# One more block product split in seven, in the last two groups of a mixture-of-ranks kernel

## What is computed

```python
x2 = einsum('bct,bcd->bdt', x, weights[condition])        # 64x64 matrix chosen per b
xf = x2.reshape(-1, 1024)                                 # 4096 rows
scores = xf @ Wr.T                                        # 64 experts
top_vals, top_idx = top_k(scores, 16)
G = scatter(softmax(top_vals), top_idx)                   # 4096 x 64, 16 non-zero
h = einsum('nd,krd->nkr', xf, A)                          # 4096 x 1024
out = einsum('nkr,kdr->nd', h * G[:, :, None], B)         # 4096 x 1024
return x + 2.0 * out
```

## Time and profile before

| what | value |
|---|---|
| median of 3 runs | 707.24 us |
| the profiled execution | 707.46 us, its span 705.7 us |
| TensorE busy | 700.4 us, 99% |
| VectorE busy | 568.8 us, 81% |
| ScalarE busy | 292.2 us, 41% |
| granted TensorE clock | 0.999 of full |
| HBM traffic | 306 GB/s over the span |

### The profile page before, as it was taken

The page is one execution under the profiler, slowest core; times in us unless marked ns, Lnnn a source line. Parts: engine busy times, 40 slices in busy tenths (PEclk is TensorE's granted clock), DMA queues, the critical chain, the costliest instruction groups (busy, mean ns, idle before and its releaser), DMA issues.

```text
span 705.7 us, 11098 instructions
## 1 busy us (share of the span) xinstructions
PE 700.4 (99%) x3822; PEld 608.5 (86%) x3822; DVE 568.8 (81%) x1022; ACT 292.2 (41%) x541; POOL 15.8 (2%) x22
## 2 busy tenths in 40 slices
PE   8999999999999999999999999999999999999998
PEld 8888888888888888988999888898899988888897
DVE  5888998897757899889795867987668496699885
ACT  5575554534535541444333542242334364233220
POOL 0000000100000000010000000001000000000100
PEclk9999999999999999999999999999999999999999
DMA  8976679787899998979989775868769987666886
GB/s 314 405 291 279 211 281 401 229 261 268 332 382 417 415 359 290 406 255 325 388 312 412 285 271 189 301 247 245 248 274 372 380 311 258 199 217 211 228 329 239
DMA packets 68937, 212.35 MB, mean 301 GB/s; under 512 B 10706, under 2 KB 13394, under 8 KB 68242
## 3 DMA queue, kind: packets, MB, share of 16 engines
q1 hardware_dynamic: 64802, 204.30, 78.0%
q0 software_dynamic: 2304, 4.20, 3.9%
q10 hardware_dynamic: 1776, 3.15, 1.2%
HBM read 150.80 MB, written 65.01 MB: 306 GB/s over the span
## 4 chain that ended last, share of the span: by engine, by line
PE 99%; DMA 1%; DVE 0%; issue 0%; DVEq 0%
PE Pb L755 40%; PE Pb L788 29%; PE Pb L809 13%; PE Cb L737 8%; PE S L852 4%; PE Pb L831 3%; DMA xc<-in_wts 1%; PE S L844 1%; PE T L907 0%; PE T L913 0%; PE Pb L771 0%; PE Cb L866 0%; PE S L866 0%; PE T L866 0%; DVE Q L1212 0%
## 5 line engine op out<-in xcount | busy, mean ns | idle before, releaser
L755 PE MATMUL Pb<-Op,Wt 128*128 128x512 f32 x888 | 214.2, 391 | 0.0
L755 PEld LDWEIGHTS Pb<-Op,Wt 128*128 128x128 f32 x888 | 165.4, 188 | 33.9
L788 PE MATMUL Pb<-Wt,Op 128*128 128x512 f32 x744 | 179.7, 391 | 0.0
L788 PEld LDWEIGHTS Pb<-Wt,Op 128*128 128x128 f32 x744 | 138.1, 188 | 28.1 <-DVE Op L1212 0.4
L1212 DVE TENSOR_TENSOR Q<-Pb,Q 128x512 f32<-128x512 f32 (+1 forms) x105 | 92.8, 901 | 27.9 <-issue 17.5
L1212 DVE TENSOR_TENSOR Op<-R,Op 128x512 fp32r<-128x512 f32 x100 | 66.6, 686 | 23.4 <-ACT Op L945 23.3
L755 PE MATMUL Pb<-Ox,Wt 128*128 128x512 f32 x300 | 75.3, 390 | 0.0
L998 ACT COPY R<-Cb 128x512 f32<-128x512 f32 x60 | 35.1, 587 | 91.2 <-PE Cb L737 91.2
L755 PEld LDWEIGHTS Pb<-Ox,Wt 128*128 128x128 f32 x300 | 56.0, 188 | 11.5
L945 ACT CAST Op<-R 128x512 fp32r<-128x512 f32 x100 | 58.3, 622 | 17.3 <-DVE R L1212 10.4
L1212 DVE TENSOR_TENSOR Cq<-Pb,Cq 128x1024 f32<-128x1024 f32 (+1 forms) x46 | 44.5, 966 | 24.3 <-issue 10.4
(11 more groups left out here) (118 smaller groups left out, 688.9 us busy)
## 6 DMA issues: line engine op xcount, KB each, us to landing
Wt<-Wd SPq DMA_DIRECT2D x201, 512.0 KB, 6.5
Wd<-Wt SPq DMA_DIRECT2D x56, 512.0 KB, 5.1
xc<-in_x SPq DMA_DIRECT2D x24, 512.0 KB, 5.4
Q<-in_x SPq DMA_DIRECT2D x16, 512.0 KB, 5.3
out<-Q SPq DMA_DIRECT2D x8, 1024.0 KB, 4.8
BR<-in_B SPq DMA_DIRECT2D x4, 1024.0 KB, 8.5
Q<-in_x SPq DMA_DIRECT2D x16, 256.0 KB, 5.6
out<-in_x SPq DMA_DIRECT2D x16, 256.0 KB, 5.9
```

Source lines behind the costliest of these rows:

```text
L755: t = e.matmul(Pb[:, j, :], Wt[:, k, a, 128 * c:128 * c + 128], part((USES1[m], s, c), z), start=fresh and (c, a, z) == (0, 0, 0), stop=(c ...
L788: t = e.matmul(Pb[:, i, :], part((USES2[m], s, c), a)[:, 128 * i:128 * i + 128], Wt[:, k, z, :], start=fresh and (c, a, z) == (0, 0, 0), s ...
```

## The change

P4 in groups 2 and 3 is made as seven products of 256 x 256 x 256 (`FOUR`, `four`). Its operand T4 gets the seven forms: the four sums are written to `u` in stage P6 (`sum_y` with `four`), and there are seven T4 splits instead of four, two of them in stage P4. Its seven weights (level 8) are made in group 2's first half, from a further load of A into `raws[2]` in group 1's last stage. Since the seven products take over the banks that hold P7's values, VectorE first adds these to the result in `base_four` (two banks after P7's second step, one after its fourth, the last one with product 0), and drains all seven products (`drain_four`). The gates of q1 move from P4's steps to the first four steps of Q2. Q2's products in those groups use P2's three banks.

```diff
+FOUR = (2, 3)
+LEVEL = (4, 6, 0, 7, 8)
-           7: [8, 9, 10, 12, 13, 14, 20]}
+           7: [8, 9, 10, 12, 13, 14, 20], 8: [3, 4, 5, 6, 7, 13, 14]}
...
+    if m == 5 and s in FOUR:
+        return [("T4", k) for k in ((0,), (1, 2), (3,), (4,))[j]]
...
+    if s in FOUR:
+        return [("T4", j + 5) if j < 2 else ("G12", j - 2)]
...
+def banks_two(s, m):
+    return BANK1 if m == 0 and s in FOUR else BANK2
...
+                        if (s, m, i) == (1, 6, 0):
+                            e.wait_ge(v_made, 28)
+                            e.dma_start(raws[2], A[4:8, :, 512:1024].rearrange("j p n -> p j n")).then_inc(l_b[4], 16)
...
+                if m == 0 and s in FOUR and k in (0, 1, 3):
+                    if k:
+                        e.wait_ge(*{1: (v_p2, p4_done(s, 5)), 3: (v_prod["P4"], 4 * s + 2)}[k])
+                    else:
+                        e.wait_ge(v_p2, p4_done(s, 4))
...
+            def four(s, k):
+                n = used_first(s, 6, k)
+                at = n % NW
+                e.wait_ge(v_lo["T4"], t4_done(s, k))
+                e.wait_ge(l_t[at], w_landed(n))
+                e.wait_ge(v_p2, p4_done(s, {0: 1, 1: 1, 2: 3, 3: 3, 4: 6, 5: 7, 6: 8}[k]))
+                for j in range(2):
+                    for c in range(2):
+                        for a, z in ((0, 0), (0, 1), (1, 0)):
+                            t = e.matmul(Pb[:, BANK2[k], 256 * j:256 * j + 256],
+                                         Wt[:, at, a, 256 * j + 128 * c:256 * j + 128 * c + 128],
+                                         part(("T4", s, k), z)[:, c, :],
+                                         start=k in (0, 1, 3) and (j, c, a, z) == (0, 0, 0, 0),
+                                         stop=(c, a) == (1, 1), skip_group_check=True)
+                t.then_inc(p_two, 1)
...
+                if name == "t1" and four:
+                    e.wait_ge(v_t4, s + 2)
+                    e.wait_ge(v_lo["S4"], split_done("S4", s - 1, 6))
+                    if s == 2:
+                        e.wait_ge(*stored(8, 3))
+                        e.wait_ge(*stored(8, 6))
...
+            def drain_four(s, r):
+                e.wait_ge(p_two, form_done(s, 8, r))
+                e.wait_ge(v_p2, p4_done(s, {0: 1, 1: 3, 2: 5, 3: 4, 4: 7, 5: 6, 6: 8}[r]))
+                P, to = Pb[:, BANK2[r], :].rearrange("p (j n) -> p j n", n=256), first2(r, 0)
+                if r < 5:
+                    add(to, P, to, v_p2)
+                else:
+                    add(to, P, to, v_prod["P4"], n=2)
+                if r == 0:
+                    add(Cq[:, 0, 3, :], Pb[:, 3, :], Cq[:, 0, 3, :], v_p2)
+
+            def base_four(s, j):
+                if j == 1:
+                    e.wait_ge(a_prod["P1"], 4 * s + 4)
+                    add(Cq[:, 0, 0:2, :], Pb[:, 0:2, :], Cq[:, 0, 0:2, :], v_p2)
+                elif j == 3:
+                    add(Cq[:, 0, 2, :], Pb[:, 2, :], Cq[:, 0, 2, :], v_p2)
...
+                            if s in FOUR:
+                                sum_y(s, SUMS2[j], True)
...
-                            gated(s, 3, j, 1)
-                            if s:
+                                if name == "G12":
+                                    lo(name, s, c)
+                            if j < 4:
+                                gated(s, 3, j, 1)
+                            if s and s not in FOUR:
                                 gated(s, 1, j, 0)
...
-                        if m or s not in ONE:
+                        if m == 6 and s in FOUR:
+                            drain_four(s, j)
+                        elif m or s not in ONE:
                             drain_first(s, m, j)
+                        if m == 5 and s in FOUR:
+                            base_four(s, j)
...
                             if m == 0 and c < 4:
                                 gated(s, 0, c, 0)
+                                if s in FOUR:
+                                    gated(s, 1, c, 0)
```

More of the change, by code:

```diff
@@ L79, in steps_first @@
 def steps_first(s, m):
-    return 7 if m == 0 and s in ONE else 4
+    return 7 if m == 0 and s in ONE or m == 6 and s in FOUR else 4
 def step_first(m, j):
@@ L93, in first_use, with fours @@
 def first_use(m):
-    return min(s for s in range(NS) if (s in ONE if m == 7 else m in TWO[s]))
+    return min(s for s in range(NS) if (s in ONE if m == 7 else s in FOUR if m == 8 else m in TWO[s]))
 def ones(s):
     return sum(r in ONE for r in range(s))
+def fours(s):
+    return sum(r in FOUR for r in range(s))
 def cond_step(s, m, i):
@@ L179, in places @@
                     spare.extend(at["y21", s, c] for c in ((0, 1, 5, 6, 7) if j == 6 else (j,) if FORMS[j][0] == "t" else ()))
+                elif m == 6 and s in FOUR:
+                    spare.append(at["T4", s, j])
                 elif j == 3:
@@ L206, in tile_done @@
 def tile_done(s, m, j):
-    return 49 * s + 7 * m - 7 * ones(s + (m > 0)) + (j + 1 if j < 3 else 7)
+    return 49 * s + 7 * m - 7 * ones(s + (m > 0)) - 7 * fours(s) + (j + 1 if j < 3 else 7)
 def chunk_done(s, m, c):
@@ L225, in form_done @@
 def form_done(s, m, k):
-    return 7 * (ones(s) if m == 7 else ones(s + 1)) + 7 * (level_before(s, TWO[s][0]) if m == 7 else level_before(s, m)) + k + 1
+    of_first = ones(s + (m != 7)) + fours(s + (m < 7))
+    return 7 * of_first + 7 * level_before(s, TWO[s][0] if m > 6 else m) + k + 1
 def level_before(s, m):
@@ L237, in y21_done, with t4_done, ysum_done, p2_done @@
     return 4 * s + 4 * ones(s) + c + 1
+def t4_done(s, k):
+    return 4 * s + 3 * fours(s) + k + 1
+def ysum_done(s, name, four):
+    return 4 * (ones(s + four) + fours(s)) + SUMS2.index(name) + 1
+def p2_done(s, n):
+    return 3 * ones(s) + 8 * fours(s) + n
+def p4_done(s, n):
+    return 3 * ones(s + 1) + 8 * fours(s) + n
+def banks_two(s, m):
+    return BANK1 if m == 0 and s in FOUR else BANK2
 def split_done(name, s, c):
@@ L420, in weight2 @@
             c, n = [(0, 0), (1, 0), (1, 1), (0, 0), (0, 1), (1, 0), (1, 1)][k]
-            if m == 7:
+            if m > 6:
                 c, n = n, c
@@ L470, in source @@
                 return quarter(y(1, 0, 4) if FORMS1[c][0] == "b" else Cq[:, 3, :, :], FORMS1[c])
+            if name == "T4" and s in FOUR:
+                return quarter(y(1, 0, 4) if FORMS[c][0] == "b" else u[:, :, :], FORMS[c])
             if name == "S2":
@@ L507, in operand_used @@
                 return (p_score, 7 * s + 1) if FORMS1[c][0] == "b" else (p_two, form_done(s, 7, c))
+            if name == "T4" and s in FOUR:
+                return p_two, form_done(s, 8, c)
             if name in USES1:
@@ L521, in bank_read @@
             if not second and m == 1 and s in ONE:
-                return ((v_p2, 3 * ones(s) + 1), (v_out, out_done(s - 1, 6, 6)), (v_p2, 3 * ones(s) + 3),
+                return ((v_p2, p2_done(s, 1)), (v_out, out_done(s - 1, 6, 6)), (v_p2, p2_done(s, 3)),
                         (a_prod["P2"], 4 * s + 4))[j]
@@ L527, in bank_read @@
                 m, second = (6, False) if second else (m - 1, False)
+            if second and m == 0 and s in FOUR:
+                return ((v_prod["P4"], 4 * s + 4) if j == 1 else in_output(s, 0, {0: 1, 2: 5, 3: 6}[j]))
             if second and m in TWO[s]:
@@ L650, in _ @@
                                 made_store(k, MADE_AT[k].index(step - 1))
+                        if s == 2 and step - 1 in MADE_AT[8]:
+                            made_store(8, MADE_AT[8].index(step - 1))
                         if (s, step) == (1, 9):
@@ L824, in one @@
                 elif k == 6:
-                    e.wait_ge(v_p2, 3 * ones(s) + 2)
+                    e.wait_ge(v_p2, p2_done(s, 2))
                 else:
@@ L880, in _ @@
                                 score_pieces(s)
+                            continue
+                        elif m == 6 and s in FOUR:
+                            four(s, j)
                             continue
@@ L1020, in wait_y21 @@
                 else:
-                    e.wait_ge(v_ysum, 4 * ones(s) + SUMS2.index(FORMS1[c]) + 1)
+                    e.wait_ge(v_ysum, ysum_done(s, FORMS1[c], False))
             def hi_first(name, s, c):
@@ L1038, in hi_first @@
                     e.wait_ge(v_t3, s + 1)
+                elif name == "T4" and s in FOUR and FORMS[c][0] == "t":
+                    e.wait_ge(v_ysum, ysum_done(s, FORMS[c], True))
                 elif name == "T4":
@@ L1128, in _ @@
                                 made_hi(k, MADE_AT[k].index(step))
+                        if s == 2 and step in MADE_AT[8]:
+                            made_hi(8, MADE_AT[8].index(step))
                         if m == 0 and s in ONE:
@@ L1411, in drain_first @@
                     if s in ONE:
-                        e.wait_ge(v_p2, 3 * ones(s + 1))
+                        e.wait_ge(v_p2, p2_done(s, 3))
                     to = Cq[:, 1, j + 1 - n:j + 1, :]
@@ L1498, in _ @@
```

(2 more changed lines are left out.)

47 lines of the change are left out of this document (28 added, 19 removed).

## The result

The changed kernel takes 717.99 us, the median of four runs (717.61 to 718.91), against 707.72 us of the kernel before in the same comparison: a ratio of 1.0149, with a 95% interval of 1.0134 to 1.0164. The profiled execution took 718.16 us with a span of 716.4 us.

A forecast was written before the change was run, and what follows sets the result against it. TensorE's instruction stream was taken to bound the kernel. Group 2 +3.6, group 3 +4.7 and early group 2 +0.1 made +8.4 us on the profiled 707.46; median 0.2 lower, 715.6 us, range 711 to 720.

The forecast's parts named there:

- Bound and direction: Whole kernel: TensorE's stream is the time, 1.6 us of columns to gain, new waits cost more; slower given 0.92.
- the price read from P2: P4's seven products priced by P2's row: 84 narrow matmuls in 10.08 us, 1.44 us per product.
- P4's walk: P4, groups 2 and 3: VectorE's queue added up operation by operation; stage 14.52 us, 3.62 us more per group.
- The forecast stalls: P4: TensorE waits for drains before products 2, 4 and 5, of 2.1, 1.9 and 0.35 us.
- Q2 of group 3: q1's gates delay drain 4, so product 6 stalls 1.1 us; no stall in group 2.
- Making seven weights: Group 2's first half: added splits and sums push P1's second drain; value 0.05 us, bounds 0 and 0.5.
- Stores, the load of A and the units: Added DMA traffic hides behind SyncE's nine-unit, 13 us lead against 10.1 us landing; value 0, bounds 0 and 1 us.
- The clock: Rival: idle gaps in P4 drop TensorE to the 1.2 GHz level; about 725 us, chance 0.06.
- The rival's price: Clock rival in P4: products 2 to 6 all slow, 14.4 us, +5 us per group.
- The sum: Whole kernel: group 2 +3.6, group 3 +4.7, early part of group 2 +0.1, together +8.4 us, giving 715.6 us.

The follow-up runs named there:

- Experiment 5: Changed kernel, A loaded early, most of VectorE's splits, sums, gates and base additions around P4 cut to about 8 columns, drains whole: 706.16 us, ratio 0.998.
- experiment 1: Changed kernel with the 1 MB load of A issued earlier, in group 1's Q5 stage instead of Q3: 716.92 us.
- experiment 8: Kernel before plus only the 1 MB load of A at group 1's Q3 start, into a buffer nobody reads: 709.19 us, ratio 1.0026.
- experiment 3: Changed kernel with q1's gates put back into P4's first four steps: 724.12 us, ratio 1.0231.
- experiment 4: Changed kernel with each product's drain placed ahead of that step's split, sum and gate in P4's VectorE order: 718.63 us.
- experiment 6: Changed kernel with the early load of A and q1's and q3's gates of groups 2 and 3 on GpSimd instead of VectorE: 719.98 us.

## Why the prediction came out as it did

**Bound and direction.** Right. TensorE's stream was the time, 1.6 us of columns was all there was to gain, and the first waits in mid-run cost more. Experiment 5 measured the gain with VectorE's other work taken away: stages of 10.08 us, which is the price read from P2.

**P4's walk.** Right in mechanism and place, small in size: +3.62 us per group were forecast, +3.91 and +3.94 came. The drains started where the walk put them, so the earlier restarts do not add up. What was mis-sized is the last one, behind drain 3. The walk let product 5 begin 0.07 us after that drain's end; in group 3 it begins 0.15 us after (634.26 to 634.41). From there to the stage's end the two products take 3.11 us, not 2.88: the first behind a pause takes 1.51 us to the next start (as 627.80 to 629.31), and the last matmul ends 0.16 us after the next stage's could start. The forecast stalls were 2.1, 1.9 and 0.35 us; group 3 has 2.23, 1.70 and about 0.3, the last inside the row of 36 matmuls. In group 2 the slow clock fills most of the second.

**Q2 of group 3.** +1.07 forecast, +1.36 measured, and none in group 2, as forecast. The same restart makes the difference: product 6 begins 0.15 us after its drain's end and takes 1.66 us to the stage's end.

**Making seven weights.** The push of P1's second drain was forecast at 0.05 us with bounds of 0 and 0.5; it is 0.3 us. The drain starts 9.67 us into P5, where the walk had 9.66; what was mis-sized is again the time from a drain's end to the matmul behind it.

**Stores, the load of A and the units.** This is the step that failed. It took the landing time of a stretch without the load (10.1 us) against a lead of 13 us and said 0, with 1 us as bound. Both sides were off. The row beside it already had the queue at 103% of the engines: in such a stretch an added megabyte delays what follows by its own length, some 2.5 us at 411 GB/s, and the units landed after 12.3 us. And nine buffers lead by eight products, 11.5 us, since a buffer is free only when its product has ended. Experiments 1 and 8 give 1.7 to 1.8 us for it. I also looked for late weights in P4 and Q2, where the new product is, and not in P2, where the load was added.

**The clock.** Given 0.06, at about 725 us. It did happen, in part: the clock fell to the lower level behind the stall of group 2. It cost nothing in the stages, as drain 2 was later still, and that is luck rather than foresight: the prediction had no such argument, and in experiments 3, 4 and 6 a fall cost time. The rival's price let all of products 2 to 6 run slow, which no run showed; in experiment 3, with stalls of 2.8 and 2.9 us, the fall is worth 2.6 us per group less the 0.9 that it hides, in experiment 6, with one stall of 4.7 us, at most 2.5 and 1.5.

**The sum.** 715.6 us forecast, 717.99 measured, inside the range of 711 to 720. As a difference it is 8.4 us against 10.3 in the medians (the kernel before took 707.72 in that comparison, not 707.24). The stages account for more than the gap of 1.9: 1.8 the load, 0.6 the two P4 stages, 0.3 Q2 and 0.25 P5, 3.0 in all, against a start of the profiled execution that is 0.6 shorter for no reason shown; the remaining 0.5 is within the scatter of the medians.

## What to carry to other kernels

Where one engine is busy throughout, a change that saves its instructions must be checked at each engine that has to answer it within one product: write down that engine's queue from the last event fixed by the busy engine and add up start to start. It is the work that is queued ahead of each answer that counts, not the engine's share of the span. And a transfer added where the DMA engines are full delays those behind it by about its own length, so put it where the share is below one, even if it is wanted later; count the lead of a prefetch from the end of the product that frees the buffer.

## What the hardware showed that was not expected

- The TensorE clock fell to 0.50 behind a stall of 2.2 us in group 2, and did not in group 3 behind the same stall; in experiment 1 it fell in both groups. With stalls of 2.8 and 2.9 us in a row it fell in both groups of the profiled execution, only in the second stall, and products 4 to 6 took 7.11 and 7.17 us instead of 4.55. What decides it is open.
- A GpSimd multiplication of 128x512 from SBUF takes 1.27 us with VectorE idle and up to 4.35 us beside VectorE's SBUF operations (experiment 6; such spans are rough). It can also stretch VectorE's operations on two SBUF operands from 0.68 to as much as 1.77 us; drains from PSUM keep their 1.21 us.
